# The last encoder layer of a fused decoder kernel: the third norm of a tile split, its halves put behind other work

## The reference, cut to what matters

```python
def _L1_attn_ref(x, ...):                      # x: (16, 112, 256)
    xb = jnp.transpose(x, (1, 0, 2))
    for l in range(4):
        ...                                    # q, k, v; masked softmax over 16 keys; o; output projection
        xb = _layernorm(xb + o, g1[l], be1[l])             # first norm
        ff = jax.nn.relu(jnp.einsum('bsd,fd->bsf', xb, W1[l]) + b1[l])
        ff = jnp.einsum('bsf,df->bsd', ff, W2[l]) + b2[l]
        xb = _layernorm(xb + ff, g2[l], be2[l])            # second norm
    return jnp.transpose(xb, (1, 0, 2))

x = _layernorm(x + _L1_attn_ref(x, ...))                   # third norm, of the residual sum
x = _layernorm(x + _L1_xattn_ref(x, ctx_768, ...))
x = _layernorm(x + _L1_ffn_ref(x, ...))
```

## Time and profile before

| what | value |
|---|---|
| median of 3 runs | 2401.41 us |
| the profiled execution's own time | 2396.02 us |
| its span in the profile | 2394.2 us |
| PE busy | 2103.9 us (88% of the span) |
| DVE busy | 1514.4 us (63%) |
| ACT busy | 711.3 us (30%) |
| POOL busy | 810.4 us (34%) |
| chain that ended last, by engine | PE 64%, DVE 25%, POOL 6%, issue 3%, ACT 2% |

### The profile page before, as it was taken

One profiled execution on the slowest core, in us unless ns is written; L12 is line 12 of the kernel. 1 busy time (PEld: TensorE's weight loads), 2 busy tenths in 40 slices (PEclk: granted clock), 3 DMA queues, 4 the chain that ended last, 5 costly groups with the idle time before them and its releaser, 6 DMA issues.

```text
span 2394.2 us, 37754 instructions
## 1 busy us (share of the span) xinstructions
PE 2103.9 (88%) x15300; PEld 1469.6 (61%) x15300; DVE 1514.4 (63%) x3047; ACT 711.3 (30%) x1407; POOL 810.4 (34%) x726
## 2 busy tenths in 40 slices
PE   6988979999999978999999999988567767879986
PEld 2334337777766656888888888776445555446632
DVE  7998955566333325556556555666398998737556
ACT  6445324333311222232223222222142222121132
POOL 3242448966500014444444444432270000013101
PEclk9768689999899989999999999999766675889998
DMA  5222173222010027101001000100231110310001
GB/s 154 70 75 90 57 161 92 60 67 71 7 53 1 1 94 173 34 1 69 1 2 51 19 1 1 52 1 1 71 100 29 30 30 25 87 49 1 0 0 31
DMA packets 67181, 114.47 MB, mean 48 GB/s; under 512 B 34153, under 2 KB 58722, under 8 KB 65794
## 3 DMA queue, kind: packets, MB, share of 16 engines
q1 hardware_dynamic: 67010, 112.07, 16.3%
HBM read 91.56 MB, written 33.34 MB: 52 GB/s over the span
## 4 chain that ended last, share of the span: by engine, by line
PE 64%; DVE 25%; POOL 6%; issue 3%; ACT 2%; DMA 0%; SPq 0%; DVEq 0%; POOLq 0%; ACTq 0%
PE PS L1534 8%; PE PS L1550 8%; PE PS L1280 5%; PE PS L1258 4%; DVE top L2334 4%; DVE w_s L2343 4%; PE PS L2214 2%; DVE ln_st L270 2%; PE PS L2204 2%; PE PS L1447 2%; PE PS L1461 2%; PE PS L2143 2%; PE PS L892 2%; PE PS L879 2%; PE PS L409 2%
## 5 line engine op out<-in xcount | busy, mean ns | idle before, releaser
L289 POOL TENSOR_SCALAR ln_ve<-ln_mv 128x2 f32<-128x2 f32 (+1 forms) x87 | 20.0, 230 | 1195.5 <-DVE ln_mv L273 1195.4
L1807 POOL TENSOR_TENSOR q_x<-q_f,cols 128x2048 f32<-128x2048 f32 x56 | 217.9, 3911 | 9.7 <-ACT q_f L1638 8.0
L1762 DVE TENSOR_TENSOR p_x<-PS,cols 128x1024 f32<-128x1024 f32 x112 | 129.3, 1218 | 134.3 <-PE PS L1496 134.3
L1089 DVE TENSOR_REDUCE XD<-PS 112x2 f32<-112x750 f32 x128 | 120.0, 940 | 96.0 <-PE PS L879 95.6
L457 PE MATMUL PS<-bc_parts,ident 96*128 96x448 bf16 x256 | 106.0, 518 | 41.2 <-DVE st_h L691 28.0
L1048 ACT ACTIVATE e_t<-PS 125x672 f32<-125x672 f32 x128 | 93.5, 730 | 154.8 <-PE PS L892 154.8
L1337 DVE SCALAR_TENSOR_TENSOR XA<-PS,gate_w,XA 112x256 f32<-112x256 f32 x128 | 56.0, 480 | 125.6 <-PE PS L1280 125.6
L2096 PE MATMUL PS<-dg,e_p 112*125 112x112 f32 x384 | 80.1, 400 | 61.7 <-ACT dg L2292 61.7
L1625 ACT ACTIVATE wb<-PS,cols 128x256 f32<-128x256 f32 x224 | 90.8, 472 | 142.8 <-PE PS L1534 142.8
L879 PE MATMUL PS<-enc_w,q_s 32*112 32x375 f32 x512 | 130.6, 535 | 1.7 <-DVE XD L1089 1.7
L892 PE MATMUL PS<-q_s,enc_w 32*125 32x112 f32 x1536 | 121.9, 289 | 2.6 <-ACT e_t L1048 2.6
(11 more groups left out here) (366 smaller groups left out, 4710.6 us busy)
## 6 DMA issues: line engine op xcount, KB each, us to landing
k_full_scratch<-k_scratch SPq DMA_DIRECT2D x112, 112.0 KB, 2.9
v_all_scratch<-v_st SPq DMA_DIRECT2D x16, 750.0 KB
v_t<-v_all_scratch SPq DMA_DIRECT2D x16, 750.0 KB
t_ring<-k_full_scratch SPq DMA_DIRECT2D x8, 784.0 KB, 12.4
enc_w<-in_enc_w SPq DMA_DIRECT2D x2, 3072.0 KB, 11.2
wc<-in_enc_w SPq DMA_DIRECT2D x2, 3072.0 KB, 12.2
k_all_scratch<-k_st SPq DMA_DIRECT2D x16, 375.0 KB
enc_w<-k_all_scratch SPq DMA_DIRECT2D x64, 93.8 KB, 3.5
```

Of the source, the lines that this page charges most:

```text
L1089: dve.tensor_reduce(nm_w[0:T, g % 4, 64 * half + 16:64 * half + 49:32], PS[0:T, 2 * half:2 * half + 2, 0:S2], AX.X, ALU.max, negate=True). ...
L1762: last = dve.tensor_tensor(p_x[:, m, :, :, :], ps[1][:, m * P:(m + 1) * P].rearrange("p (h i) -> p h i", i=16).unsqueeze(2) .to_broadcast( ...
L1807: last = pool.tensor_tensor(q_x[:, c, :, :].rearrange("p t (h i) -> p t h i", i=16), q_f[:, k % 2, c, :].rearrange("p (t i) -> p t i", i=1 ...
```

## The change

The third norm of the last layer's jobs is cut in two. `last_stats(i)` (residual sum, bn_stats, bn_aggr) stands on DVE behind the first norm of the same step; `last_apply(i)` (the two tensor_scalars, which signal `n2_done`) stands in the next step behind the values' bias v_z and ahead of p_x. `turn_second` of these jobs moves on PE from behind the scores to between the two halves of `feed_in`, and ACT's two copies of it (`copy_last`) to between the two halves of the relus. Job 27, the last, keeps the old places. POOL's roots follow DVE's order. No instruction is added or removed.

```diff
+        LAST_0 = STEPS - ROUNDS
 ...
-                if 0 <= k - 3 < STEPS and k != STEPS + 1:
+                if 0 <= k - 3 < LAST_0 or k == STEPS + 2:
                     turn_second(k - 3)
 ...
-                if k == STEPS + 1:
-                    turn_second(k - 3)
                 if 0 <= k - 2 < STEPS:
                     feed_in(k - 2, 0)
+                    if LAST_0 <= k - 3:
+                        turn_second(k - 3)
                     feed_in(k - 2, 1)
 ...
                 if 0 <= k - 2 < STEPS:
                     relu(k - 2, 0)
+                    if LAST_0 <= k - 3:
+                        copy_last(k - 3)
                     relu(k - 2, 1)
 ...
-                    affine(layer, x, "g2", "be2", None)
-                    link(dve.tensor_tensor(x, x, xg0[:, 2 * r:2 * r + 2, :], ALU.add))
-                    normed(x).then_inc(n2_done, 1)
+            def last_stats(i):
+                r = i % ROUNDS
+                x = xg[:, 2 * r:2 * r + 2, :]
+                link(dve.tensor_tensor(x, x, xg0[:, 2 * r:2 * r + 2, :], ALU.add))
+                return norm_stats(dve, link, [x[:, g, :] for g in range(2)], P)
+
+            def last_apply(i, k):
+                r = i % ROUNDS
+                for g in range(2):
+                    x = xg[:, 2 * r + g, :]
+                    last = norm_apply(dve, k, g, x, x, P)
+                last.then_inc(n2_done, 1)
 ...
+                if LAST_0 <= k - 3 < STEPS:
+                    last_apply(k - 3, waiting)
                 if 0 <= k - 1 < STEPS:
                     dve.wait_ge(et_ready, k)
 ...
+                if LAST_0 <= k - 2:
+                    waiting = last_stats(k - 2)
+            last_apply(STEPS - 1, waiting)
 ...
-                    if k - 2 >= STEPS - ROUNDS:
-                        norm_root(pool, link, 2, P)
                 if 0 <= k - 1 < STEPS and k != STEPS:
+                    norm_root(pool, link, 2, P)
+                if LAST_0 <= k - 2 < STEPS:
                     norm_root(pool, link, 2, P)
```

More of the change, by code:

```diff
@@ L1617, in copy_residuals, with copy_last @@
                         .then_inc(xg0_copied, 1)
+            def copy_last(i):
+                r = i % ROUNDS
+                act.wait_ge(ez_ready, i + 1)
+                for c in range(KC):
+                    last = act.copy(
+                        XF[:, c, :].rearrange("p (b t) -> p t b", b=B)[:, 16 * r:16 * r + 16, :],
+                        ps[3][:, c * RT:(c + 1) * RT].rearrange("p (t b) -> p t b", b=B))
+                last.then_inc(ez_copied, 1)
             def relu(i, half):
@@ L1645, in enc_act @@
                     act.copy(s_t[:, :], ps[0]).then_inc(st_copied, 1)
-                if 0 <= k - 3 < STEPS:
-                    layer, r = divmod(k - 3, ROUNDS)
+                if 0 <= k - 3 < LAST_0:
+                    r = (k - 3) % ROUNDS
                     act.wait_ge(ez_ready, k - 2)
[L1649 to L1657, removed]
+                    act.copy(XD[:, :, r * RT:(r + 1) * RT], ps[3].rearrange("p (c n) -> p c n", c=KC))\
+                        .then_inc(ez_copied, 1)
+                if k == STEPS + 2:
+                    copy_last(k - 3)
                 if k < STEPS:
@@ L1710, in second_norm @@
                 link(normed(x))
-                if layer < LAYERS - 1:
-                    affine(layer, x, "g2", "be2", n2_done)
-                else:
-                    affine(layer, x, "g2", "be2", None)
-                    link(dve.tensor_tensor(x, x, xg0[:, 2 * r:2 * r + 2, :], ALU.add))
-                    normed(x).then_inc(n2_done, 1)
+                affine(layer, x, "g2", "be2", n2_done if layer < LAYERS - 1 else None)
+            def last_stats(i):
[4 more added lines that the diff above has]
+            def last_apply(i, k):
+                r = i % ROUNDS
+                for g in range(2):
+                    x = xg[:, 2 * r + g, :]
+                    last = norm_apply(dve, k, g, x, x, P)
+                last.then_inc(n2_done, 1)
             def first_norm(i):
@@ L1727, in first_norm @@
                 affine(layer, x, "g1", "be1", n1_done)
+            waiting = None
             for k in range(STEPS + 2):
```

## The result

The changed kernel takes 2411.44 us, the median of five runs (2407.98 to 2418.05), against 2401.41 before. The ratio is 1.005 with a 95% interval of 1.0033 to 1.0066: 8 to 16 us slower. The forecast was 2416.8 us, with 2399 to 2424 as its range. The profiled execution's span is 2408.6 us against 2394.2, 14.4 us more.

A forecast was written before the change was run, and what follows sets the result against it. The last layer was taken as bound by a closed PE-DVE loop, with the third norm on its path. Four rounds losing 26.8 us less 11.4 gained in steps 28 and 29 gave +15.4 on 2401.41: 2416.8 us, range 2399 to 2424.

The forecast's parts named there:

- What is removed: Last layer's round: third norm leaves the path ahead of the first norm, x1's transposes start 3.14 us earlier, at +10.62.
- The multiply: DVE's softmax multiply, steps 24 to 27: starts at +15.63 under POOL's q_x, waits for it and ends at +18.98.
- The tensor_scalars wait for POOL: DVE's last_apply, steps 24 to 27: waits for the second q_x instruction and ends at +23.35; +20.4 without waiting.
- The wait and the rest of the round: PE, steps 24 to 27: idles some 7 us inside feed-in; round 34.96 us at full clock, 4.4 us longer.
- The clock: PE after its wait, steps 24 to 27: a lower granted clock adds 2.3 us a round, bounds 0 and 3.
- Steps 28 and 29: Last two steps, without q_x: gains of 4.0 and 7.4 us, together 11.4, bounds 5.9 and 11.4.
- The sum: Whole kernel: 26.8 us lost over four rounds less 11.4 gained, +15.4 us, bounds +6.2 and +23.7.
- The first rival: DVE's last_apply, steps 24 to 27: tensor_scalars don't wait for POOL; round 31.97 us, kernel 2395.6 us; chance 0.12.
- The prediction's reading by duration: DVE's tensor_scalars: two of 256 elements take 0.74 us, two bn_stats 0.75, so no doubled rate and no wait for POOL.

The follow-up runs named there:

- last_apply early: Changed kernel with last_apply moved on DVE from behind v_z to between the softmax's subtraction and its row sum; 2384.14 us, 0.9942 of the kernel before.
- PE busy in the wait: Changed kernel with 14 more matmuls on PE between the first half of feed-in and the turn, steps 24 to 27; 2401.72 us, 1.0012 of the kernel before.
- The sum in PSUM: Changed kernel with last_stats writing the residual sum to PSUM bank 3, where last_apply reads it; 2399.06 us, 0.9998 of the kernel before.
- q_x in quarters: Changed kernel with POOL's q_x in four instructions of 1024 elements instead of two of 2048; 2403.03 us in one run.
- tail-only kernel: Changed kernel with the split kept for jobs 25 to 27 alone, jobs 21 to 24 as before the change; 2383.15 us, 0.9941 of the kernel before.

## Why the prediction was right

The mechanism, the place and the sign were as forecast, and the terms of the sum too, with small errors. That the sum is only 1 us off is in part luck, since the errors have both signs.

- *What is removed*: 3.14 us a round; x1 is done at about +10.65 (L1723 starts at +10.57, and each next instruction is recorded 0.08 us ahead of the end of the one before where nothing links them), foretold +10.62.
- *The multiply*: foretold to run from +15.63 to +18.98; it ran from +15.43 to +18.88.
- *The tensor_scalars wait for POOL*: yes, to +22.90. Foretold was +23.35, too large by 0.45. Most of that is the 0.81 us of the earlier trace rows from POOL's end to the pair's end: in step 29 the tensor_scalar that waited ended 0.50 us behind POOL's instruction, under q_x 0.16, and the pair 0.48 us behind. What makes that difference is not shown. Reading that row as a wait of the pair, and not of its first instruction alone, made the early `last_apply` look better than it is.
- *The wait and the rest of the round*: 6.41 us of idle PE for some 7; the round without the clock 34.54 (PE busy in the wait) for 34.96.
- *The clock*: 2.51 us a round for 2.3. The prediction put 0.3 us on the transposes, where its own rows give 1.12 against 0.66, that is 0.46. It differs from round to round: the second half of feed-in takes 5.17 us in the first and 6.09 in the last, so the first round is 36.49 us and the mean 37.05.
- *Steps 28 and 29*: 11.55 for 11.4. Their shares were not 4.0 and 7.4. `weigh` came 28.17 us behind the zero, a gain of 4.3, but by another way: PE was to wait for `last_apply` at the full clock, and in fact the first half of feed-in was slow (5.41 us, granted clock 0.50), PE got to the turn at +16.8, and `last_apply` was done at +16.3. The clock's loss filled the time in which PE would have waited, so that the 4.0 came out near by luck. Step 29 gave 7.2.
- *The sum*: +14.4 in the profiled executions for +15.4, +10.0 in the medians, +8 to +16 by the ratio. The median lies 5.4 us under the forecast. Of that 1.0 is the sum. The rest comes from the 5.4 us that was added because the profiled execution before was faster than its median by so much; that of the changed kernel was only 1.1 us faster.
- *The first rival*, that the pair doesn't wait, is excluded in this kernel: the pair took 3.43 us. The sum in PSUM made it true by another way: the rival's round was 31.97, or more with some clock lost, and that run measured 33.70 with a clock that fell.
- The Trainium skill's page "SBUF — State Buffer", section "Who interferes with whom", gives the exclusion for a whole instruction, and the trace agrees: the wait went with the length of POOL's instructions (the pair was done at +22.9 with q_x in two instructions and at +21.0 with it in four), and with a PSUM source there was none. The same section counts tensor_scalar among the instructions that can take the shared pair, so by itself it did not speak for the first rival. The prediction's reading by duration, that a tensor_scalar as long as a bn_stats keeps clear of POOL, does not hold here: it took 0.41 us alone and 3.11 under q_x.

## What to carry to other kernels

When work is taken off the path and put into a later step, look up what POOL runs there at that moment, and not only whether the engine has room: an SBUF-to-SBUF tensor_scalar of 0.4 us cost 3 us behind a q_x instruction, and PE, queued behind it, stood idle for 6.4 us and then ran part of feed-in at half clock. Two cures were shown, and they add up (a round of 37.05 us went to 33.70 by the first, 31.10 by the second, 27.89 by both): put the intermediate sum into PSUM, so that the instruction that reads it no longer waits for POOL, and place that instruction so early that its result is there when PE arrives. A change with a gaining and a losing part should be run part by part; the gaining part here, alone, made the kernel 0.6% faster, 9.4 us of it (0.4%) in the encoder.

## What the runs showed of the hardware that was not expected

**Turns go one instruction at a time, to whoever waits.** Engines do not wait for each other on semaphores only, as the opening has it: the multiply's wait for q_x stands in the rows as a longer duration (3.45 us, 0.69 alone), with no idle time and no releaser in brackets, and neither instruction waits for a semaphore of the other's engine. Of two adjacent tensor_scalars the second can lose the turn (1.28 and then 3.78 us, last_apply early), so a pair under two POOL instructions may pay twice (1.36 and 2.02 us with q_x in quarters).

**A float32 tensor_scalar with two per-partition scalars** is as long from SBUF as a bn_stats (0.41 and 0.42 us for 256 elements), and yet it waits for POOL: its length alone doesn't show that it will. From PSUM a pair takes 0.98 to 1.00 and not 0.74 us, whether POOL runs or not.

**The stretch behind the encoder has two lengths.** The code there is the same in all kernels. From its first `MAX8` on `w_s` to the last, before the change and then in the tail-only kernel (starts of first and last are the last two times ahead of the shapes):

```profile
L2334 DVE MAX8 top<-w_s x192: 534/544/554, 1735.6 to 2046.1; 112x8 f32<-112x375 f32 x192
```

```profile
L2358 DVE MAX8 top<-w_s x192: 530/540/547, 1726.4 to 2030.7; 112x8 f32<-112x375 f32 x192
```

That is 310.5 against 304.3 us. The difference, 6.2 us, is one batch. Of the 16, most take 18.4 us, but one in the tail-only and the last_apply-early kernel, and two in the seven others, are longer by 6.2 us (a distance of 15.6 us between two groups of `MAX8` that are otherwise 9.4 apart). In the first such batch of the kernel before, PE's granted clock stayed at half. In all, the stretch behind the last zero was 3.9 us shorter in the tail-only kernel and 3.7 us in the last_apply-early one than before, which is why these two gained more in their profiled executions than the encoder explains. Whether the place in time of the encoder's end decides it, or chance, was not tested.
